# LSTM steps on one core: the residual of h from one scan over threes, whole h of four steps multiplied by GpSimd

## The chip, the cores and the metric

One core of one Trainium2 chip runs the whole program. The metric is the device time of one execution in microseconds (us); smaller is better. The output has the shape of x, 4 sequences of 1024 positions with 512 features.

## What is computed

Four blocks follow one another, each with a residual addition: a sparsifier, an LSTM, a gated recurrence that works by cumulative sums, and a second LSTM. The two LSTMs are the same code with other weights; the change touches them alone.

```python
def step(carry, xw_t):            # both LSTMs, 1024 steps, batch 4, H = 512
    prev_h, prev_c = carry
    a = xw_t + prev_h @ Wh        # Wh: 512 x 2048
    i = sigmoid(a[:, :H]); f = sigmoid(a[:, H:2*H])
    o = sigmoid(a[:, 2*H:3*H]); g = tanh(a[:, 3*H:])
    next_c = f * prev_c + i * g
    next_h = o * tanh(next_c)
    return (next_h, next_c), next_h
x = x + sparsify(x, cond)
x = x + lstm(x, cond, Wx1, Wh1, b1)
x = x + gated_scan(x, cond, ...)
x = x + lstm(x, cond, Wx3, Wh3, b3)
```

## The kernel before

**Layout.** Features lie on the 128 partitions. A hidden vector h of 512 features and 4 sequences is therefore 4 chunks of 128 features by 4 columns: 16 columns. The products run in float16 on TensorE, and to keep precision each value is split into two float16 numbers, a high part and a residual ("low") part. Both Wh and h are split so.

**One step.** The 512 hidden units are handled in two halves, A (chunks 0 and 1, `first`) and B (chunks 2 and 3, `second`), so that the engines can overlap. The gates of a half stand in a PSUM bank each (`PA`, `PB`). The h products (`h_product`, line 404) load h as the stationary operand, 8, 16, 24 or 32 columns in the four steps of a group, and stream 256 columns of Wh. Four matmuls, one for each group of 32 array columns, run beside one another.

TensorE takes, in each step, the products of A's part of h (16 matmuls for gates A, then 12 for gates B), then waits for B's part of h (semaphore `h_b`), then 16 for gates A, which completes them (`gates_a`), and 20 for gates B (`gates_b`), and last some products of x for the following group of four steps (line 397). It starts a step when A's part of h is there (`h_a`).

VectorE (DVE) then turns the gates from PSUM by 32x32 transposes (line 593) into feature order, adds the high and the low row (`both_parts`, line 598), multiplies (`multiply`, line 601), and makes c (`new_c`, line 604). ScalarE (ACT) makes tanh of g, i and f (lines 492 and 499), sigmoid of o (495 and 502), and tanh of c (497 and 504). Then DVE has three operations for each half:

```python
whole_h:  HH  = sig_o * tanh_c                    # float32, line 611
high_h:   hi  = float16(sig_o * 128 * tanh_c)     # line 614
low_h:    lo  = float16(HH * 128 - hi)            # line 619, signals h_a or h_b
```

`sig_o` is a float32 tile in SBUF and `tanh_c` one in PSUM, both contiguous and each one step deep. `H` holds, for every chunk, the 32 float16 columns that the matmul loads, side by side.

**Order of the work.** It is written out by hand, engine by engine, and each engine takes its list in order. On DVE, the operations of A and B are interleaved: `whole_h` and `high_h` of A stand between the second transpose of B and `multiply` of B, and `low_h` of A stands behind the addition of B's o gate.

**Groups of four steps.** A bank holds the gates of four steps (V = 4). After each group GpSimd (POOL) adds whole h of the four steps to x (line 384) and then prepares the float16 parts of x for a later group (`parts_of_x`, lines 350, 351 and 354). HH is double-buffered over groups. A loop round has two groups (eight steps); 128 rounds make the 1024 steps of an LSTM.

Of the kernel before, what the change touches and what calls it, by code (L numbers as in the profile page):

```python
# [250 lines left out]
def lstm(nc, m, tag, x_all, weights, wh, b, wh_there, also_load=()):  # L251
# [7 lines left out]
    with ExitStack() as ctx:  # L259
        s = Sems(nc, ctx, tag, "bias biasd biasp exponent usual sxb xh xscaled xhi xw sq vmax root prep zero br0 ones amaxk amax amaxall cond dbl hi lo next "  # L260
                               "gates_a tr_a to_a pre_a preo_a g_a pr_a c_a tc_a hi_a h_a "
                               "gates_b tr_b to_b pre_b preo_b g_b pr_b c_b tc_b hi_b h_b xadd "
# [4 lines left out]
        H = sbt("H", [P, V, NC, Q], F16)  # L267
        HH = sbt("HH", [P, 2, V, NC * B])
# [18 lines left out]
        class Half:  # L287


            def __init__(self, name, chunk):  # L290
# [13 lines left out]
                self.tanh_c = pst("TC" + name)[:, 0:M]  # L304
                self.sig_o = sbt("SIGO" + name, [P, M])
# [40 lines left out]
        def _(pool):  # L346
# [167 lines left out]
        def _(dve):  # L514
            nc.vector.memset(first.c, 0.0).then_inc(s["zero"], 1)
            nc.vector.memset(second.c, 0.0).then_inc(s["zero"], 1)
            nc.vector.memset(H[:], 0.0).then_inc(s["zero"], 1)
# [103 lines left out]

            with dve.Fori(0, ROUNDS) as r:
                for v in range(2):
                    for u in range(V):
# [296 lines left out]
```

## Time and profile before

| | |
|---|---|
| median of 3 runs | 7913.7 us (7913.2 to 7918.02) |
| the profiled execution's own time | 7913.46 us |
| its span, first to last instruction | 7911.4 us |
| PE busy | 5366.3 us (68%), 169280 matmuls |
| DVE busy | 5627.1 us (71%), 37427 instructions |
| ACT busy | 2281.7 us (29%) |
| POOL busy | 842.9 us (11%) |
| DMA | 37.24 MB, 5 GB/s over the span |

The span is what the profiler saw between the first instruction and the last; 2.06 us of the execution's time lie outside it. PE is the stream of matmuls and PEld the weight loads, which overlap it. Names that begin with p_ belong to the first LSTM and those with q_ to the second; `p_PREA` is A's gates in feature order, `p_GBA` holds A's tanh values and c, `p_PRA` its products, `p_SIGOA` and `p_TCA` its sigmoid of o and tanh of c. DVE and ACT overlap an instruction with the one before it, so an instruction's duration is longer than the distance between two starts. A wait is shown in square brackets or behind a bar, with what ended it.

### The profile page before, as it was taken

To read this page: it belongs to the slowest core of one execution; us is meant where nothing else is said; L and a number is where in the kernel's file an instruction comes from. 1 tells how busy PE (TensorE), PEld (TensorE's weight loads), DVE (VectorE), ACT (ScalarE), POOL (GpSimd) and SP (SyncE) were. 2 spreads that over 40 slices of the span, in tenths; PEclk is the share of its full clock that TensorE was granted. 3 is DMA by queue.
4 is the path that set the end of the run, shared out by engine and by line. 5 is a ranking of instruction groups with operands and counts; after the bars stand their busy time and mean duration, and the time that the engine had idled before them with its cause. 6 is when DMAs were issued, how large, how long until landed. Compare 5 with 4: busy or idle time off the path is not lost. (4 is left out here: it accounts for less than half of the span.)

```text
span 7911.4 us, 404450 instructions
## 1 busy us (share of the span) xinstructions
PE 5366.3 (68%) x169280; PEld 4157.3 (53%) x169280; DVE 5627.1 (71%) x37427; ACT 2281.7 (29%) x12741; POOL 842.9 (11%) x2143
## 2 busy tenths in 40 slices
PE   1566666666666666666983666666666666666666
PEld 1455555555555555555431555555555555555555
DVE  7777777777777777777678777777777777777776
ACT  4322222222222222222354222222222222222222
POOL 5100000000000000000013000000000000000000
PEclk5899999999999999999996999999999999999999
DMA  2000000000000000000001000000000000000001
GB/s 85 17 0 0 0 0 0 0 0 0 0 0 0 0 0 0 0 0 0 0 0 43 0 0 0 0 0 0 0 0 0 0 0 0 0 0 0 0 0 43
DMA packets 32261, 37.24 MB, mean 5 GB/s; under 512 B 6112, under 2 KB 22496, under 8 KB 32224
## 3 DMA queue, kind: packets, MB, share of 16 engines
q1 hardware_dynamic: 32224, 36.76, 1.4%
q8 instruction: 21, 0.34, 0.0%
q14 instruction: 16, 0.13, 0.0%
HBM read 28.34 MB, written 8.39 MB: 5 GB/s over the span
## 5 line engine op out<-in xcount | busy, mean ns | idle before, releaser
L404 PE MATMUL q_PA<-scratch,q_H 128*8 128x256 f16 (+1 forms) x32768 | 1255.2, 273 | 1071.8 <-DVE q_H L619 1071.8
L404 PE MATMUL p_PA<-scratch,p_H 128*8 128x256 f16 (+1 forms) x32768 | 1254.9, 273 | 1071.8 <-DVE p_H L619 1071.8
L404 PEld LDWEIGHTS q_PA<-scratch,q_H 128*8 128x8 f16 (+1 forms) x32768 | 649.7, 90 | 1494.2 <-DVE q_H L619 1359.7
L404 PEld LDWEIGHTS p_PA<-scratch,p_H 128*8 128x8 f16 (+1 forms) x32768 | 649.0, 90 | 1494.6 <-DVE p_H L619 1359.6
L404 PE MATMUL q_PB<-scratch,q_H 128*8 128x256 f16 (+1 forms) x32768 | 1249.7, 273 | 0.0
L404 PE MATMUL p_PB<-scratch,p_H 128*8 128x256 f16 (+1 forms) x32768 | 1249.4, 273 | 0.0
L593 DVE STREAM_TRANSPOSE q_GT<-q_PA 128x192 f32<-128x192 f32 (+1 forms) x2048 | 526.0, 295 | 747.7 <-PE q_PA L404 747.7
L593 DVE STREAM_TRANSPOSE p_GT<-p_PA 128x192 f32<-128x192 f32 (+1 forms) x2048 | 526.5, 295 | 746.7 <-PE p_PA L404 746.7
L404 PEld LDWEIGHTS q_PB<-scratch,q_H 128*8 128x8 f16 (+1 forms) x32768 | 834.5, 92 | 59.8
L404 PEld LDWEIGHTS p_PB<-scratch,p_H 128*8 128x8 f16 (+1 forms) x32768 | 833.5, 92 | 60.8
L492 ACT ACTIVATE q_GBA<-q_PREA 128x24 f32<-128x24 f32 x1024 | 194.7, 190 | 1900.9 <-DVE q_PREA L598 1900.9
L492 ACT ACTIVATE p_GBA<-p_PREA 128x24 f32<-128x24 f32 x1024 | 194.9, 190 | 1900.3 <-DVE p_PREA L598 1900.3
L593 DVE STREAM_TRANSPOSE q_GT<-q_PB 128x192 f32<-128x192 f32 (+1 forms) x2048 | 639.5, 312 | 0.0
L593 DVE STREAM_TRANSPOSE p_GT<-p_PB 128x192 f32<-128x192 f32 (+1 forms) x2048 | 639.4, 312 | 0.0
L384 POOL TENSOR_TENSOR xb<-xb,q_HH 128x64 f32 x256 | 81.9, 320 | 3172.4 <-DVE q_H L619 3172.4
L384 POOL TENSOR_TENSOR xa<-xa,p_HH 128x64 f32 x256 | 81.6, 319 | 3172.7 <-DVE p_H L619 3172.7
L736 PE MATMUL g_z<-xa,scratch 128*128 128x512 f32 x768 | 351.6, 619 | 45.4 <-DVE scratch L788 43.5
L598 DVE TENSOR_TENSOR p_PREB<-p_GT 128x24 f32<-128x24 f32 (+1 forms) x2048 | 361.7, 177 | 0.0
L598 DVE TENSOR_TENSOR q_PREB<-q_GT 128x24 f32<-128x24 f32 (+1 forms) x2048 | 361.5, 177 | 0.0
L619 DVE SCALAR_TENSOR_TENSOR p_H<-p_HH,p_H 128x8 f16<-128x8 f32 x2048 | 334.4, 163 | 35.4
L619 DVE SCALAR_TENSOR_TENSOR q_H<-q_HH,q_H 128x8 f16<-128x8 f32 x2048 | 334.2, 163 | 35.4
L598 DVE TENSOR_TENSOR q_PREA<-q_GT 128x24 f32<-128x24 f32 (+1 forms) x2048 | 359.3, 175 | 0.0
(220 smaller groups left out, 9390.6 us busy)
## 6 DMA issues: line engine op xcount, KB each, us to landing
scratch<-in_x_dram SPq DMA_DIRECT2D x8, 1024.0 KB, 5.4
out_dram<-xa SPq DMA_DIRECT2D x16, 512.0 KB, 6.1
xb<-in_L_cond_Wx_dram SPq DMA_DIRECT2D x8, 384.0 KB, 6.8
xb<-in_L_cond_Wh_dram SPq DMA_DIRECT2D x8, 384.0 KB, 6.7
xa<-in_L_cond_Wx_dram SPq DMA_DIRECT2D x8, 384.0 KB, 5.9
xa<-in_L_cond_Wh_dram SPq DMA_DIRECT2D x8, 384.0 KB, 6.1
xb<-in_L_cond_Wx_dram SPq DMA_DIRECT2D x8, 128.0 KB, 7.0
xb<-in_L_cond_Wh_dram SPq DMA_DIRECT2D x8, 128.0 KB, 6.8
```

The source lines that it names most:

```text
L384: nc.gpsimd.tensor_tensor(here, here, HH[:, v].rearrange("p u (c b) -> p c u b", b=B), ALU.add).then_inc(s["xadd"], 1)
L404: last = nc.tensor.matmul(half.banks[buf][Q * j:Q * j + rows, 0:GA * Q], H[:, u, k, 0:rows], w16[:, part, k, j, half_cols(half)], start=False,
L492: nc.scalar.activation(first.tanhs, first.pre_gif.rearrange("p (n m) -> p n m", n=3), ACT.Tanh, scale=half_scale).then_inc(s["g_a"], 1)
L593: return nc.vector.transpose(GT[:, lo:hi, :].rearrange("p g n -> p (g n)"), half.banks[v][:, (lo - half.at) * Q:(hi - half.at) * Q])
L598: return nc.vector.tensor_tensor(by_unit(dst), GT[:, lo:hi, at:at + B], GT[:, lo:hi, at + B:at + 2 * B], ALU.add)
L619: return nc.vector.scalar_tensor_tensor(nxt[:, :, B:2 * B], by_unit(HH[:, v, u, half.cols]), H_SCALE, nxt[:, :, 0:B], ALU.mult, ALU.subtract)
L736: last = nc.tensor.matmul(banks[w * 2 + n % 2][:], wt[:, w, k, c * P:(c + 1) * P], m.xa[:, k, blk * TBB:(blk + 1) * TBB], start=(k == 0), ...
```

## The change

`sig_o` and `tanh_c` of eight steps now lie in one float32 SBUF tile `SO`, in threes: for each column a zero, sigmoid of o and tanh of c. ACT writes sigmoid and tanh into it, 4 bytes at a time with 12 and 24 bytes between them. `H` becomes a tile `HP` of float16 threes, where the third place holds h and the first place of the high half a constant -128. `high_h` reads `SO` in place of a tile in SBUF and one in PSUM. `low_h` becomes one scan over 24 elements, with state = data0 * state - data1: over a three, it gives 128, then 128 times sigmoid of o, then that times tanh c minus the high part, which is the residual. So it no longer needs `HH`, and `whole_h` is gone from DVE. GpSimd multiplies sigmoid and tanh of the four steps of a group in one instruction and then adds as before. The matmul loads the stationary columns with 12 bytes between them.

```diff
+        HP = sbt("H", [P, 2, V, V, 2, B, NF, 3], F16)
+        SO = sbt("SO", [P, U, 2, B, NF, 3])
+        HH = sbt("HH", [P, V, NC * B])
...
-                self.tanh_c = pst("TC" + name)[:, 0:M]
-                self.sig_o = sbt("SIGO" + name, [P, M])
+                self.n = chunk // NF
+                self.sig_o, self.tanh_c = (SO[:, :, self.n, :, :, e].rearrange("p u b c -> p u c b") for e in (1, 2))
...
-                    nc.gpsimd.tensor_tensor(here, here, HH[:, v].rearrange("p u (c b) -> p c u b", b=B), ALU.add).then_inc(s["xadd"], 1)
+                    nc.gpsimd.tensor_tensor(HH[:].rearrange("p u (h c b) -> p (u h) b c", h=2, b=B),
+                                            *(SO[:, v * V:(v + 1) * V, :, :, :, e].rearrange("p u h b c -> p (u h) b c") for e in (1, 2)), ALU.mult).then_inc(s["whole"], 1)
+                    pool.wait_ge(s["whole"], done)
+                    nc.gpsimd.tensor_tensor(here, here, HH[:].rearrange("p u (c b) -> p c u b", b=B), ALU.add).then_inc(s["xadd"], 1)
...
-                    last = nc.tensor.matmul(half.banks[buf][Q * j:Q * j + rows, 0:GA * Q], H[:, u, k, 0:rows],
+                    last = nc.tensor.matmul(half.banks[buf][Q * j:Q * j + rows, 0:GA * Q], HP[:, k // NF, u, 0:u + 1, :, :, k % NF, 2].rearrange("p u s b -> p (u s b)"),
...
-            nc.vector.memset(H[:], 0.0).then_inc(s["zero"], 1)
+            nc.vector.memset(HP[:].rearrange("p h s u t b c e -> p (h s u t b c) e")[:, :, 0], -H_SCALE).then_inc(s["zero"], 1)
+            nc.vector.memset(HP[:].rearrange("p h s u t b c e -> p (h s u t b c) e")[:, :, 1:3], 0.0).then_inc(s["zero"], 1)
...
-            def whole_h(half, v, u):
-                return nc.vector.tensor_tensor(HH[:, v, u, half.cols], half.sig_o[:], half.tanh_c, ALU.mult)
-
-            def high_h(half, u):
-                return nc.vector.scalar_tensor_tensor(next_h(half, u)[:, :, 0:B], by_unit(half.sig_o[:]), H_SCALE, by_unit(half.tanh_c),
-                                                      ALU.mult, ALU.mult)
+            def high_h(half, v, u):
+                at, here = v * V + u, (u + 1) % V
+                return nc.vector.scalar_tensor_tensor(HP[:, half.n, here, here, 0, :, :, 2].rearrange("p b c -> p c b"), half.sig_o[:, at], H_SCALE,
+                                                      half.tanh_c[:, at], ALU.mult, ALU.mult)
             def low_h(half, v, u):
-                nxt = next_h(half, u)
-                return nc.vector.scalar_tensor_tensor(nxt[:, :, B:2 * B], by_unit(HH[:, v, u, half.cols]), H_SCALE, nxt[:, :, 0:B],
-                                                      ALU.mult, ALU.subtract)
+                here = (u + 1) % V
+                threes = lambda a: a.rearrange("p b c e -> p (b c e)")
+                return nc.vector.tensor_tensor_scan(threes(HP[:, half.n, here, here, 1]), threes(SO[:, v * V + u, half.n]),
+                                                    threes(HP[:, half.n, here, here, 0]), 0.0, ALU.mult, ALU.subtract)
```

**On DVE**, in a step from B's second transpose on, before:

```order
L593 STREAM_TRANSPOSE p_GT<-p_PB 128x64
L611 TENSOR_TENSOR p_HH<-p_SIGOA,p_TCA 128x8 [waits p_tc_a]
L614 SCALAR_TENSOR_TENSOR p_H<-p_SIGOA,p_TCA 128x2x4
L601 SCALAR_TENSOR_TENSOR p_PRB<-p_GBB 128x16 [waits p_g_b]
L598 TENSOR_TENSOR p_PREB<-p_GT 128x8 [waits p_to_b]
L619 SCALAR_TENSOR_TENSOR p_H<-p_HH,p_H 128x2x4 [waits p_hi_a]
L604 SCALAR_TENSOR_TENSOR p_GBB<-p_PRB 128x8 [waits p_pr_b]
L611 TENSOR_TENSOR p_HH<-p_SIGOB,p_TCB 128x8 [waits p_tc_b]
L614 SCALAR_TENSOR_TENSOR p_H<-p_SIGOB,p_TCB 128x2x4
L619 SCALAR_TENSOR_TENSOR p_H<-p_HH,p_H 128x2x4 [waits p_hi_b]
```

and with the change, where `p_SO` is the tile of threes:

```order
L600 STREAM_TRANSPOSE p_GT<-p_PB 128x64
L615 SCALAR_TENSOR_TENSOR p_H<-p_SO 128x2x4 [waits p_tc_a]
L608 SCALAR_TENSOR_TENSOR p_PRB<-p_GBB 128x16 [waits p_g_b]
L605 TENSOR_TENSOR p_PREB<-p_GT 128x8 [waits p_to_b]
L622 SCALAR_TENSOR_TENSOR p_H<-p_SO,p_H 128x24 [waits p_hi_a]
L611 SCALAR_TENSOR_TENSOR p_GBB<-p_PRB 128x8 [waits p_pr_b]
L615 SCALAR_TENSOR_TENSOR p_H<-p_SO 128x2x4 [waits p_tc_b]
L622 SCALAR_TENSOR_TENSOR p_H<-p_SO,p_H 128x24 [waits p_hi_b]
```

The two multiplications of line 611 are gone, and the rest keeps its places. The last instruction of each half, line 619 before and line 622 now, is printed under one name, but is the scan of 24 elements.

**On GpSimd**, at the end of a group of four steps, before:

```order
L384 ISA [waits p_h_b,p_h_a]
L384 TENSOR_TENSOR xa<-xa,p_HH 128x4x16
L350 ISA [waits p_xh,p_xw]
L350 TENSOR_TENSOR p_XC<-xa,p_SXB 128x64
L351 TENSOR_TENSOR p_XH<-xa,p_SXB 128x16x4
```

and with the change:

```order
L387 TENSOR_TENSOR p_HH<-p_SO 128x8x4x2 [waits p_h_b,p_h_a]
L390 ISA [waits p_whole]
L390 TENSOR_TENSOR xa<-xa,p_HH 128x4x16
L353 ISA [waits p_xh,p_xw]
L353 TENSOR_TENSOR p_XC<-xa,p_SXB 128x64
L354 TENSOR_TENSOR p_XH<-xa,p_SXB 128x16x4
```

One instruction is added ahead of the addition to x, it waits for both halves of h, and the addition waits for it. Everything behind, the three instructions that prepare x, comes later by what these take.

## Rows read from the trace of the kernel before

**Rows 1.** Page, groups: count | busy us, mean ns | idle us before

```profile
L593 DVE STREAM_TRANSPOSE p_GT<-p_PA 128x192 f32<-128x192 f32 (+1 forms) x2048 | 526.5, 295 | 746.7 <-PE p_PA L404 746.7
```

**Rows 2.** DVE timeline, one step: start us, us, instruction [idle before <-releaser]

```profile
2003.39 0.51 DVE L593 STREAM_TRANSPOSE p_GT<-p_PA 128x192 f32<-128x192 f32 x2 [0.73 <-PE p_PA L404]
2003.83 0.17 DVE L598 TENSOR_TENSOR p_PREA<-p_GT 128x24 f32<-128x24 f32 x1
...
2004.46 0.17 DVE L604 SCALAR_TENSOR_TENSOR p_GBA<-p_PRA 128x8 f32<-128x8 f32 x1
...
2004.88 0.16 DVE L611 TENSOR_TENSOR p_HH<-p_SIGOA,p_TCA 128x8 f32<-128x8 f32 x1
...
2005.03 0.17 DVE L601 SCALAR_TENSOR_TENSOR p_PRB<-p_GBB 128x16 f32<-128x16 f32 x1
...
2005.19 0.16 DVE L619 SCALAR_TENSOR_TENSOR p_H<-p_HH,p_H 128x8 f16<-128x8 f32 x1
2005.27 0.16 DVE L604 SCALAR_TENSOR_TENSOR p_GBB<-p_PRB 128x8 f32<-128x8 f32 x1
2005.67 0.16 DVE L611 TENSOR_TENSOR p_HH<-p_SIGOB,p_TCB 128x8 f32<-128x8 f32 x1 [0.25 <-ACT p_TCB L504]
...
2005.95 0.17 DVE L619 SCALAR_TENSOR_TENSOR p_H<-p_HH,p_H 128x8 f16<-128x8 f32 x1
2006.83 0.52 DVE L593 STREAM_TRANSPOSE p_GT<-p_PA 128x192 f32<-128x192 f32 x2 [0.72 <-PE p_PA L404]
```

**Rows 3.** Timeline of ACT, the same step

```profile
2004.66 0.18 ACT L497 ACTIVATE p_TCA<-p_GBA 128x8 f32<-128x8 f32 x1
2004.78 0.18 ACT L499 ACTIVATE p_GBB<-p_PREB 128x24 f32<-128x24 f32 x1
...
2005.46 0.18 ACT L504 ACTIVATE p_TCB<-p_GBB 128x8 f32<-128x8 f32 x1
```

**Rows 4.** Timeline of PE, from the start of the next products

```profile
2005.41 0.61 PE L404 MATMUL p_PA<-scratch,p_H 128*8 128x256 f16 x16 [1.09 <-DVE p_H L619]
...
2006.17 0.61 PE L404 MATMUL p_PA<-scratch,p_H 128*8 128x256 f16 x16
```

**Rows 5.** The line of a scan: count, duration ns min/median/max

```profile
L803 DVE TENSOR_TENSOR_SCAN xb<-one,scratch x16: 2292/2294/5972, 3916.7 to 4261.5; 128x1024 f32<-128x1024 f32 x16
```

**Rows 6.** Weight loads by form, 2000 to 3000 us

```profile
L404 PEld LDWEIGHTS p_PB<-scratch,p_H 128*32 128x32 f16 x2304 | 61.6, 97 | 1.2
...
L404 PEld LDWEIGHTS p_PB<-scratch,p_H 128*8 128x8 f16 x2304 | 55.9, 87 | 7.0
```

**Rows 7.** Timeline of PEld, 16 bytes between columns

```profile
7891.79 4.33 PEld L828 LDWEIGHTS s_tp<-ident,xb 128*128 128x128 f32 x35
```

**Rows 8.** Timeline of PEld, contiguous columns

```profile
3799.91 1.78 PEld L725 LDWEIGHTS g_z<-ident,scratch 128*128 128x128 f32 x16
```

**Rows 9.** Groups of ACT, SBUF to SBUF

```profile
L759 ACT ACTIVATE g_LC<-g_LC 128x1024 f32<-128x1024 f32 x16 | 16.9, 1058 | 0.5
...
L487 ACT ACTIVATE p_one_sig<-eps 128x1 f32<-128x1 f32 x1 | 0.2, 203 | 0.0
```

**Rows 10.** Timeline of POOL behind the step of rows 2

```profile
2006.35 0.32 POOL L384 TENSOR_TENSOR xa<-xa,p_HH 128x64 f32 x1 [12.31 <-DVE p_H L619]
...
2006.91 0.32 POOL L351 TENSOR_TENSOR p_XH<-xa,p_SXB 128x64 f16<-128x64 f32 x1
2007.38 0.32 POOL L354 TENSOR_TENSOR p_XH<-p_XC,p_XH 128x64 f16<-128x64 f32 x1
```

**Rows 11.** Timeline of POOL, the next group of four steps

```profile
2020.97 0.32 POOL L351 TENSOR_TENSOR p_XH<-xa,p_SXB 128x64 f16<-128x64 f32 x1
```

**Rows 12.** Timeline of DVE beside rows 11

```profile
2020.64 0.52 DVE L593 STREAM_TRANSPOSE p_GT<-p_PA 128x192 f32<-128x192 f32 x2 [0.72 <-PE p_PA L404]
2021.07 0.26 DVE L598 TENSOR_TENSOR p_PREA<-p_GT 128x24 f32<-128x24 f32 x1
...
2024.20 0.38 DVE L593 STREAM_TRANSPOSE p_GT<-p_PA 128x192 f32<-128x192 f32 x1 [0.73 <-PE p_PA L404]
```

More of the change, by code:

```diff
@@ L261, in lstm @@
                                "gates_a tr_a to_a pre_a preo_a g_a pr_a c_a tc_a hi_a h_a "
-                               "gates_b tr_b to_b pre_b preo_b g_b pr_b c_b tc_b hi_b h_b xadd "
+                               "gates_b tr_b to_b pre_b preo_b g_b pr_b c_b tc_b hi_b h_b xadd whole "
                                + " ".join(f"wh{k}" for k in range(wh_there, NC)))
@@ L266, in lstm @@
         M = NF * B
-        H = sbt("H", [P, V, NC, Q], F16)
-        HH = sbt("HH", [P, 2, V, NC * B])
+        HP = sbt("H", [P, 2, V, V, 2, B, NF, 3], F16)
+        SO = sbt("SO", [P, U, 2, B, NF, 3])
+        HH = sbt("HH", [P, V, NC * B])
         XC = sbt("XC", [P, NC, VB])
@@ L357, in _ @@
             nc.gpsimd.memset(ONES[:], 0.0).then_inc(s["ones"], 1)
-            nc.gpsimd.memset(HH[:], 0.0).then_inc(s["xadd"], 2)
+            nc.gpsimd.memset(SO[:], 0.0).then_inc(s["xadd"], 2)
             pool.wait_ge(s["ones"], 1)
@@ L494, in steps @@
                         act.wait_ge(s["preo_a"], now)
-                        nc.scalar.activation(first.sig_o[:], first.pre_o, ACT.Sigmoid, scale=scale)
+                        nc.scalar.activation(first.sig_o[:, u], by_unit(first.pre_o), ACT.Sigmoid, scale=scale)
                         act.wait_ge(s["c_a"], now)
-                        nc.scalar.activation(first.tanh_c, first.c, ACT.Tanh, scale=0.5).then_inc(s["tc_a"], 1)
+                        nc.scalar.activation(first.tanh_c[:, u], by_unit(first.c), ACT.Tanh, scale=0.5).then_inc(s["tc_a"], 1)
                         act.wait_ge(s["pre_b"], now)
@@ L501, in steps @@
                         act.wait_ge(s["preo_b"], now)
-                        nc.scalar.activation(second.sig_o[:], second.pre_o, ACT.Sigmoid, scale=scale)
+                        nc.scalar.activation(second.sig_o[:, u], by_unit(second.pre_o), ACT.Sigmoid, scale=scale)
                         act.wait_ge(s["c_b"], now)
-                        nc.scalar.activation(second.tanh_c, second.c, ACT.Tanh, scale=0.5).then_inc(s["tc_b"], 1)
+                        nc.scalar.activation(second.tanh_c[:, u], by_unit(second.c), ACT.Tanh, scale=0.5).then_inc(s["tc_b"], 1)
             act.wait_ge(s["usual"], 1)
@@ L586, in _ @@
                 last.then_inc(s["lo"], 1)
-            dve.wait_ge(s["zero"], 3)
-            nc.vector.memset(H[:, 0, 0:NF], 0.0).then_inc(s["h_a"], 1)
-            nc.vector.memset(H[:, 0, NF:], 0.0).then_inc(s["h_b"], 1)
+            dve.wait_ge(s["zero"], 4)
+            nc.vector.memset(HP[:, 0, 0, 0, 0, :, :, 2], 0.0).then_inc(s["h_a"], 1)
+            nc.vector.memset(HP[:, 1, 0, 0, 0, :, :, 2], 0.0).then_inc(s["h_b"], 1)
             def transposed(half, v, cols):
@@ L644, in _ @@
                         dve.wait_ge(s["tc_a"], now)
-                        whole_h(first, v, u)
-                        high_h(first, u).then_inc(s["hi_a"], 1)
+                        high_h(first, v, u).then_inc(s["hi_a"], 1)
                         dve.wait_ge(s["g_b"], now)
@@ L655, in _ @@
                         dve.wait_ge(s["tc_b"], now)
-                        whole_h(second, v, u)
-                        high_h(second, u).then_inc(s["hi_b"], 1)
+                        high_h(second, v, u).then_inc(s["hi_b"], 1)
                         dve.wait_ge(s["hi_b"], now)
```

3 lines of the change are left out of this document (removed).

## The prediction

> **What bounds the kernel now.** I began with the page's groups. DVE is busy 71% of the span, yet at its first transpose of a step it sits idle for PE, 746.7 us in one LSTM's 1024 steps [rows 1], 0.73 us a step. PE has a pause of its own in every step. No engine is full: a loop bounds the kernel, and the timeline of one step shows it. DVE starts A's transpose at 2003.39 and the residual of A's h at 2005.19, ending at 2005.35 [rows 2]. PE takes that h at 2005.41 [rows 4], and its products bring the next transpose at 2006.83 [rows 2]. So a step is 1.96 us on DVE and ACT, 0.06 of handing over and 1.42 on PE, 3.44 in all; 2048 such steps make about 7050 of the span's 7911.4 us. Whatever moves the end of A's `low_h`, seen from the transpose, moves the time 2048-fold: 1 ns a step is 2 us.
>
> What sets that end? Not DVE's own list alone. ACT's tanh c of A ends at 2004.84 [rows 3], and DVE's `whole_h` starts at 2004.88 [rows 2]. The tanh for B's gates ends at 2004.96 [rows 3], and `multiply` of B starts at 2005.03 [rows 2]. The usual distance from ACT's end to DVE's start is 0.03: tanh c of B ends at 2005.64 [rows 3], `whole_h` of B starts at 2005.67 [rows 2]. So `multiply` could have begun at 2004.99. It came 0.04 late, behind `whole_h` and `high_h`.
>
> B's h is level with its need: it is ready at 2006.12, so to PE at 2006.18 [rows 2], and PE's first 28 matmuls last until 2006.17 [rows 4].
>
> **Part by part.** *`whole_h` of A goes.* Small DVE operations start 0.08 apart (2005.19 and 2005.27 [rows 2]), so 0.08 of issue goes. But `multiply` waits for ACT's tanh at 2004.99, so only 0.04 reaches it, and the addition and `low_h` behind it. Bounds: 0 where ACT's tanh comes later, 0.08 where it comes earlier. I take the gain at 0.04.
>
> *The residual becomes a scan.* A scan of 1024 elements takes at least 2292 ns [rows 5]. With a fixed part like that of the small operations (0.16 for 8 elements [rows 2], so about 0.15), it takes (2292 - 150)/1024 = 2.1 ns an element; 24 elements make 0.05, plus 0.15 is 0.20. Before it was 0.16 [rows 2]. Cost 0.04; bounds 0.03 and 0.06, the latter if the fixed part is a little larger for a scan. The next DVE operation, `new_c` of B, starts later than `low_h` by as much more, so it stays where it was, and so does tanh c of B.
>
> *Weight loads with 12 bytes between columns.* The load ahead of a step's first matmul is exposed, the others hide behind matmuls of 109 ns for four (28 in 0.76 us [rows 4]). Contiguous columns cost (97 - 87)/24 = 0.42 ns each [rows 6]. The nearest strided loads, 16 bytes apart, come one in 0.124 us (35 in 4.33), or 0.97 ns a column [rows 7], against 0.111 contiguous (16 in 1.78 [rows 8], which there the matmul sets). The difference, 0.55 ns, times a mean of 20 columns is 0.01 us a step. Bounds 0 and 0.01. The Trainium skill says otherwise ("SBUF — State Buffer", on SBUF cachelines): a stride is free up to 16 bytes, which covers both the 12 bytes here and the 16 of [rows 7]. By the rule this term would be nothing and the sum 20 us less; the row at 16 bytes contradicts it, and I go by the row.
>
> *ACT writes to SBUF, in threes.* Tanh c took 0.18 into PSUM [rows 3]. From SBUF to SBUF ACT takes 203 ns for one element and 1058 for 1024 [rows 9], so about 0.21 for 8: 0.03 more. For A, `high_h` can be 0.03 late and still end before the scan needs it. The following tanh starts 0.12 behind [rows 3]; whether this distance stays is not in the rows: between -0.01 and +0.01, and I take 0. For B: `high_h` starts 0.03 later than `whole_h` did but 0.05 earlier than `high_h` did, and the scan takes back 0.04. B's h stays level with PE's need; 0.
>
> Sum of a step: -0.04 + 0.04 + 0.01 = +0.01, **20 us** in 2048 steps. Bounds: -0.02 (-0.04, +0.03, 0 and ACT's -0.01) and +0.04 (-0.04, +0.06, +0.01, +0.01), which is -41 and +82 us.
>
> *GpSimd.* The new multiplication has 64 elements, as the addition that takes 0.32 [rows 10]; strides may make it longer. It starts once B's h is there. The addition started 0.23 behind B's h (2006.12 [rows 2], 2006.35 [rows 10]). The multiplication starts 0.03 to 0.23 behind, lasts 0.32, and the addition follows 0.23 later: it and all behind it move by 0.35 to 0.55, I take 0.45. DVE never waits for these results, since the x parts are for a later group. But there is a second coupling. In one group of four, POOL's second preparing operation starts at 2006.91, over DVE's transposes, which read PSUM [rows 10, 2]. In the next it starts at 2020.97 [rows 11], 0.33 after DVE's transpose at 2020.64, and the addition of A's gates, which reads two SBUF operands at 2021.07, takes 0.26 instead of 0.17 [rows 12, 2]. That step lasts 3.56 instead of 3.44 [rows 12, 2]. This pair alternates with the two groups of a round; so a hit costs about 0.11 and there is one in eight steps. Moved by 0.45, POOL's three operations start, from the transpose: 0.25, 0.53 and 1.00 in the one group, 0.50, 0.78 and 1.25 in the other. DVE's two-operand work runs from 0.44 (2003.83 [rows 2]) on, nearly without a gap. I count one hit in the first group (the operation at 1.00, on the work around c at 1.07) and two in the second (0.78 and 1.25). That is two hits more in eight steps: 2 x 0.11 x 256 = **56 us**. Bounds: from no hit at all (-28) to four more (+113).
>
> *Setup and tail.* DVE clears 1536 numbers instead of 256, at most 3 us an LSTM at the scan's rate and perhaps hidden; the last group's multiplication adds 0.55 at the end of each LSTM. Together 4 us (0 to 8).
>
> The sum is 20 + 56 + 4 = 80 us on the profiled execution's 7913.46, which is the median within 0.3 us: **7993 us**.
>
> **Rivals.**
>
> *The saved issue counts whole (faster).* Its place is `multiply` of B. If ACT, no longer writing tanh c to PSUM, starts B's tanh enough earlier that it ends by 2004.92, the full 0.08 is saved. The step is then 0.08 - 0.04 - 0.01 = 0.03 shorter, 61 us; with one more hit of GpSimd (28) and the setup (4) the time is 7884. It decides from where the step saves more than GpSimd adds: with 60 us there, 0.03 a step. For it: [rows 3] do not say what holds the tanh at 2004.78. Against: tanh c itself can start no earlier, since it waits for `new_c` (2004.46 to 2004.63 [rows 2], tanh at 2004.66 [rows 3]).
>
> *GpSimd's shift is harmless.* Its operations fall between DVE's, as in the group of [rows 10], and there are as many hits as before. Then 20 + 4 remain: 7937. For it: 0.25 us of shift decides in today's trace between a hit and none. Against: DVE's two-operand work is dense from 0.44 on.
>
> *A hit holds longer.* The addition at 2021.07 [rows 12] ran beside an operation that began 0.10 before it [rows 11] and lost 0.09, not the rest of that operation, 0.22. The Trainium skill ("SBUF — State Buffer", on who interferes with whom) states that the first to issue keeps the shared ports for its whole instruction and the other blocks fully. The rows show less than that. As a mechanism here: each hit costs 0.22, three hits in eight steps less the 0.11 of now make 0.55 x 256 = 141 us, so 7913 + 20 + 141 + 4 = 8078.
>
> *The four weight loads share a reader.* With 32 columns for each of four tiles, a group of four matmuls needs 128 strided columns: 0.12 us instead of 0.109 [rows 7, 4]. The 11 groups ahead of A's gates then add 0.13 in one step of four, 512 x 0.13 = 67 us: 8060. For it: nothing in the rows excludes it; against: only the widest of the four loads would reach this.
>
> *The scan does not do what it says.* A short scan may have start-up that 1024 elements hide. At 0.25 instead of 0.20 it adds 102 us: 8095.
>
> **How the numbers follow.** Chances: forecast 0.42, saved issue whole 0.17, harmless shift 0.18, longer hold 0.10, shared reader 0.08, costlier scan 0.05. A measurement of this kernel can tell 0.2%, 16 us, from no change. Slower takes the forecast nearly whole (0.40), two thirds of the harmless shift (0.11) and the last three (0.23), less a little for gains that offset them: 0.70. Faster is the first rival and a sliver of the others, 0.17; within 0.2% is 0.13. The range leaves out the costlier scan, most of the longer hold and the far side of the faster rival: 7882 to 8070. The forecast's own is 7945 to 8045.
>
> **What the profile would show.** Right: `low_h` as a scan near 0.20; `multiply` of B 0.04 sooner behind the transpose; the first matmul after h longer by up to 0.02 at 32 columns; steps 1 to 3 of a group within 0.02 of 3.44; the first step of both groups stretched, by 0.1 and 0.2, with DVE operations of 0.25 beside POOL's. Wrong: plain steps below 3.42 (the issue was the bound), first steps no longer than now (GpSimd harmless), four-matmul groups farther apart than 0.109, or a scan over 0.22.

## The result and the profile after

| | before | after |
|---|---|---|
| median of 4 runs each | 7913.99 us (7913.2 to 7918.02) | 8009.5 us (8006.59 to 8011.24) |
| ratio, 95% interval | | 1.012 [1.0108, 1.0132] |
| the profiled execution's own time, span | 7913.46, 7911.4 us | 8006.59, 8004.8 us |
| DVE instructions | 37427 | 33333 |
| first matmul on h in the first LSTM | 245.51 us | 247.37 us |

The changed kernel is slower by 95.5 us, 1.2%. DVE has 4094 instructions fewer and is busy 79 us less, and still the loop is longer. All times are of executions in the same state but one: the fourth of experiment 1 took 13980.96 us at a granted clock of 0.44 instead of 0.98, and without it the median there is 7965.5 instead of 7965.9. From the page's groups of the changed kernel:

```profile
PE 5428.4 (68%) x169280; PEld 4377.9 (55%) x169280; DVE 5547.8 (69%) x33333; ACT 2419.8 (30%) x12741; POOL 1023.9 (13%) x2655
...
L600 DVE STREAM_TRANSPOSE p_GT<-p_PA 128x192 f32<-128x192 f32 (+1 forms) x2048 | 526.4, 295 | 763.9 <-PE p_PA L410 763.9
...
L615 DVE SCALAR_TENSOR_TENSOR p_H<-p_SO 128x8 f16<-128x8 f32 x2048 | 381.9, 186 | 320.6 <-ACT p_SO L510 291.4
...
L622 DVE TENSOR_TENSOR_SCAN p_H<-p_SO,p_H 128x24 f16<-128x24 f32 x2048 | 419.4, 205 | 35.4
```

The first transpose of a step now waits 763.9 us for PE in one LSTM instead of 746.7 [rows 1]: 17 ns a step more from PE's side. The scan takes 205 ns, `high_h` 186.

One step without any disturbance, on DVE's timeline of the changed kernel (a step with 32 columns behind it, to be laid beside [rows 2]):

```profile
2009.66 0.51 DVE L600 STREAM_TRANSPOSE p_GT<-p_PA 128x192 f32<-128x192 f32 x2 [0.75 <-PE p_PA L410]
...
2011.18 0.19 DVE L615 SCALAR_TENSOR_TENSOR p_H<-p_SO 128x8 f16<-128x8 f32 x1
2011.27 0.17 DVE L608 SCALAR_TENSOR_TENSOR p_PRB<-p_GBB 128x16 f32<-128x16 f32 x1
...
2011.43 0.20 DVE L622 TENSOR_TENSOR_SCAN p_H<-p_SO,p_H 128x24 f16<-128x24 f32 x1
...
2011.98 0.19 DVE L615 SCALAR_TENSOR_TENSOR p_H<-p_SO 128x8 f16<-128x8 f32 x1 [0.28 <-ACT p_SO L510]
2012.20 0.21 DVE L622 TENSOR_TENSOR_SCAN p_H<-p_SO,p_H 128x24 f16<-128x24 f32 x1
2013.16 0.51 DVE L600 STREAM_TRANSPOSE p_GT<-p_PA 128x192 f32<-128x192 f32 x2 [0.76 <-PE p_PA L410]
```

Seen from its transpose, `multiply` of B starts at 1.61 (1.64 before), A's scan ends at 1.97 (`low_h`: 1.96), and B's scan at 2.75 (`low_h`: 2.73). The step lasts 3.50; at this width it was 3.46 before (the table below), and 3.44 in the narrower step of [rows 2]. ACT and PE in the same step:

```profile
2010.93 0.22 ACT L503 ACTIVATE p_SO<-p_GBA 128x8 f32<-128x8 f32 x1
2011.05 0.18 ACT L505 ACTIVATE p_GBB<-p_PREB 128x24 f32<-128x24 f32 x1
...
2011.72 0.22 ACT L510 ACTIVATE p_SO<-p_GBB 128x8 f32<-128x8 f32 x1
```

```profile
2011.69 0.65 PE L410 MATMUL p_PA<-scratch,p_H 128*32 128x256 f16 x16 [1.10 <-DVE p_H L622]
...
2012.49 0.62 PE L410 MATMUL p_PA<-scratch,p_H 128*32 128x256 f16 x16
```

Tanh c lasts 0.22 instead of 0.18, but the tanh behind it still starts 0.12 later, as in [rows 3]. On PE the first 28 matmuls with 32 columns last 0.80; in the same step before they took 0.78:

```profile
2001.95 0.62 PE L404 MATMUL p_PA<-scratch,p_H 128*32 128x256 f16 x16 [1.09 <-DVE p_H L619]
...
2002.73 0.61 PE L404 MATMUL p_PA<-scratch,p_H 128*32 128x256 f16 x16
```

The weight loads by form (count | busy us, mean ns | idle us before), of 2000 to 3000 us of the changed kernel: 122 ns at 32 columns and 88 at 8, where [rows 6] had 97 and 87.

```profile
L410 PEld LDWEIGHTS p_PB<-scratch,p_H 128*32 128x32 f16 x2272 | 65.3, 122 | 0.0
...
L410 PEld LDWEIGHTS p_PB<-scratch,p_H 128*8 128x8 f16 x2304 | 56.5, 88 | 6.4
```

A table over all steps between 2000 and 3000 us says it more sharply. It holds medians, in ns, of distances between starts, apart for the four widths of the next products. "h to transpose" runs from the first matmul on the new h to DVE's next transpose; B's h is the end of its last operation, counted from that matmul; so are the starts of the second and the eighth group of four matmuls (the eighth is the first that needs B's h); the last column is the period of a step, at 16 columns with the steps that GpSimd lengthens.

| columns | transpose to h matmul | h to transpose | B's h | second group of matmuls | eighth group | period |
|---|---|---|---|---|---|---|
| before, 8 | 2017 | 1426 | 707 | 109 | 764 | 3443 |
| before, 16 | 2074 | 1429 | 707 | 113 | 768 | 3503 |
| before, 24 | 2020 | 1433 | 707 | 116 | 771 | 3453 |
| before, 32 | 2020 | 1437 | 704 | 120 | 775 | 3457 |
| after, 8 | 2031 | 1442 | 716 | 116 | 772 | 3472 |
| after, 16 | 2112 | 1452 | 716 | 126 | 781 | 3561 |
| after, 24 | 2030 | 1466 | 719 | 138 | 793 | 3497 |
| after, 32 | 2031 | 1480 | 721 | 148 | 803 | 3509 |

So a plain step has three additions: about 0.01 at A's h, 0.007 to 0.028 between the first and the second group of four matmuls (the groups behind stay 109 apart: 655 from the second to the eighth at any width), and about 0.01 at B's h and the load behind it. The last shows behind the eighth group: the ninth starts 116, 117, 119 and 123 ns after it at the four widths, where it was 109 before.

What is left is GpSimd. Its timeline at the two group ends of one loop round:

```profile
2002.02 0.31 POOL L387 TENSOR_TENSOR p_HH<-p_SO 128x64 f32<-128x64 f32 x1 [11.86 <-DVE p_H L622]
2002.52 0.32 POOL L390 TENSOR_TENSOR xa<-xa,p_HH 128x64 f32 x1 [0.18 <-POOL p_HH L387]
...
2003.55 0.35 POOL L357 TENSOR_TENSOR p_XH<-p_XC,p_XH 128x64 f16<-128x64 f32 x1
...
2017.38 0.32 POOL L354 TENSOR_TENSOR p_XH<-xa,p_SXB 128x64 f16<-128x64 f32 x1
2017.85 0.36 POOL L357 TENSOR_TENSOR p_XH<-p_XC,p_XH 128x64 f16<-128x64 f32 x1
```

and DVE beside them:

```profile
2002.60 0.52 DVE L600 STREAM_TRANSPOSE p_GT<-p_PA 128x192 f32<-128x192 f32 x2 [0.72 <-PE p_PA L410]
...
2003.67 0.25 DVE L611 SCALAR_TENSOR_TENSOR p_GBA<-p_PRA 128x8 f32<-128x8 f32 x1
...
2006.16 0.51 DVE L600 STREAM_TRANSPOSE p_GT<-p_PA 128x192 f32<-128x192 f32 x2 [0.73 <-PE p_PA L410]
...
2016.63 0.51 DVE L600 STREAM_TRANSPOSE p_GT<-p_PA 128x192 f32<-128x192 f32 x2 [0.73 <-PE p_PA L410]
...
2017.50 0.23 DVE L608 SCALAR_TENSOR_TENSOR p_PRA<-p_GBA 128x16 f32<-128x16 f32 x1
```

In the one group `new_c` takes 0.25 beside POOL's last operation, in the other `multiply` 0.23 beside the one before; their neighbours in the same step keep their 0.16 to 0.18. That is two hits in eight steps, where there was one [rows 11, 12]. The multiplication lasts 0.31, and the addition starts 0.50 behind it.

### The profile page after: what moved, and what is told of

Same layout as the page of the kernel before. It is cut to its first block and busy times, and to the rows that moved or that the text cites. A ratio compares the mean times of both kernels' runs of the same rounds, so it can differ in the third digit from the quotient of the medians.

```text
span 8004.8 us, 400868 instructions
## 1 busy us (share of the span) xinstructions
PE 5428.4 (68%) x169280; PEld 4377.9 (55%) x169280; DVE 5547.8 (69%) x33333; ACT 2419.8 (30%) x12741; POOL 1023.9 (13%) x2655
## 5 line engine op out<-in xcount | busy, mean ns | idle before, releaser
L410 PEld LDWEIGHTS q_PA<-scratch,q_H 128*8 128x8 f16 (+1 forms) x32768 | 730.7, 108 | 1472.4 <-DVE q_H L622 1376.7
L410 PEld LDWEIGHTS p_PA<-scratch,p_H 128*8 128x8 f16 (+1 forms) x32768 | 730.4, 108 | 1472.2 <-DVE p_H L622 1376.6
L600 DVE STREAM_TRANSPOSE p_GT<-p_PA 128x192 f32<-128x192 f32 (+1 forms) x2048 | 526.4, 295 | 763.9 <-PE p_PA L410 763.9
L410 PEld LDWEIGHTS q_PB<-scratch,q_H 128*8 128x8 f16 (+1 forms) x32768 | 890.4, 105 | 23.2
L410 PEld LDWEIGHTS p_PB<-scratch,p_H 128*8 128x8 f16 (+1 forms) x32768 | 890.2, 105 | 23.0
L615 DVE SCALAR_TENSOR_TENSOR p_H<-p_SO 128x8 f16<-128x8 f32 x2048 | 381.9, 186 | 320.6 <-ACT p_SO L510 291.4
L615 DVE SCALAR_TENSOR_TENSOR q_H<-q_SO 128x8 f16<-128x8 f32 x2048 | 381.9, 186 | 320.5 <-ACT q_SO L510 291.4
L387 POOL TENSOR_TENSOR q_HH<-q_SO 128x64 f32<-128x64 f32 x256 | 79.5, 311 | 3079.3 <-DVE q_H L622 3079.3
L387 POOL TENSOR_TENSOR p_HH<-p_SO 128x64 f32<-128x64 f32 x256 | 79.5, 311 | 3078.6 <-DVE p_H L622 3078.6
L622 DVE TENSOR_TENSOR_SCAN q_H<-q_SO,q_H 128x24 f16<-128x24 f32 x2048 | 419.5, 205 | 35.4
L622 DVE TENSOR_TENSOR_SCAN p_H<-p_SO,p_H 128x24 f16<-128x24 f32 x2048 | 419.4, 205 | 35.4
```

The costliest lines, as they stand in the source:

```text
L387: nc.gpsimd.tensor_tensor(HH[:].rearrange("p u (h c b) -> p (u h) b c", h=2, b=B), *(SO[:, v * V:(v + 1) * V, :, :, :, e].rearrange("p u h ...
L600: return nc.vector.transpose(GT[:, lo:hi, :].rearrange("p g n -> p (g n)"), half.banks[v][:, (lo - half.at) * Q:(hi - half.at) * Q])
L615: return nc.vector.scalar_tensor_tensor(HP[:, half.n, here, here, 0, :, :, 2].rearrange("p b c -> p c b"), half.sig_o[:, at], H_SCALE, hal ...
L622: return nc.vector.tensor_tensor_scan(threes(HP[:, half.n, here, here, 1]), threes(SO[:, v * V + u, half.n]), threes(HP[:, half.n, here, h ...
```

## The experiments

Two accounts were open after this. **Mine**: a plain step costs 0.01 and GpSimd 56 us. **The other**: the plain step costs about 0.04, in tiles of threes that are slower for every engine that touches them, and GpSimd adds little. The runs take one part of the change away, or put one part into the kernel before. Each ratio is to the kernel before, timed on the same chip beside it (7912.04 for the first four, 7916.11 for the next four, 7910.2 for the last two). It moved by 6 us between these, so that a difference between kernels of two sets is good to some 5 us.

**1. The changed kernel, with contiguous weight loads**

```diff
-  HP[:, k // NF, u, 0:u + 1, :, :, k % NF, 2].rearrange("p u s b -> p (u s b)")
+  HP[:, k // NF, u].rearrange("p v s b c e -> p (v s b c e)")[:, 0:rows]
```

> The changed kernel, but TensorE loads its stationary columns side by side (the same number, other values of the same tile, so h is wrong). Theory A (strided weight loads are the largest part of the loss): in the changed kernel the second group of four matmuls follows the first of a step by 116, 126, 138 and 148 ns at 8, 16, 24 and 32 columns, against 109 to 120 before; here it is 109 to 120 again, the second exposed load (behind the wait for B's h) shrinks too, steps 1 to 3 of a group fall by 10 to 35 ns, and the time is about 7960. Rival B (the loads only look longer, the loss sits in DVE and ACT): the time stays above 7995.

Measured: 7965.88 us, ratio 1.0067 [1.0047, 1.0087]. So the strides in the weight loads cost 44 us, 0.021 a step, twice my term. The loads are back at their old 97 ns:

```profile
L410 PEld LDWEIGHTS p_PB<-scratch,p_H 128*32 128x32 f16 x2304 | 61.6, 97 | 1.2
```

and the second group starts after 109 to 120 ns as before. The distance from h to transpose is 1433 at 8 columns and 1444 at 32, still 7 longer than before: this is B's h, 715 instead of 707.

**2. The changed kernel, without GpSimd's multiplication**

```diff
-  nc.gpsimd.tensor_tensor(HH[:]..., *(SO[...] for e in (1, 2)), ALU.mult).then_inc(s["whole"], 1)
-  pool.wait_ge(s["whole"], done)
...
+  nc.gpsimd.memset(HH[:], 0.0).then_inc(s["whole"], 1)
```

> The changed kernel without GpSimd's multiplication; the addition to x adds zeros, so h is left out of the output. Theory A (GpSimd's share is small: the first step of a group grew by about as much as the other three): between 7995 and 8015, with one hit per two groups as in the kernel before. Rival C (the prediction's term: two hits more in eight steps are 56 us): about 7953.

Measured: 7992.13 us, ratio 1.0101 [1.0084, 1.0118]. Without the multiplication 17 us go, not 56, and the time is 3 us below the range that I gave. The multiplication is the small part of the loss. GpSimd's own operations are then back where they were before the change: in one group the step with 16 columns lasts 3589 ns in the mean, in the other 3480, so one group in two is hit, by 0.11, as before.

**3. The changed kernel, with the residual as an operation of 8 elements**

```diff
-  return nc.vector.tensor_tensor_scan(threes(HP[...1]), threes(SO[...]), threes(HP[...0]), 0.0, ALU.mult, ALU.subtract)
+  return nc.vector.scalar_tensor_tensor(h(1), half.sig_o[:, at], H_SCALE, h(0), ALU.mult, ALU.subtract)
```

> The changed kernel with an 8-element operation in place of the 24-element scan, with the same tiles and strides (it leaves tanh c out of the residual, so that is wrong). Theory A: low_h goes from 0.20 to about 0.16, h of A and of B both come 0.04 sooner, and the time falls by 2048 x 0.04 = 82 us to about 7928, near the kernel before: then scan and saved multiplication cancel and the rest of the loss is elsewhere. Rival D (the scan is hidden behind waits): above 7980.

Measured: 7946.96 us, ratio 1.0043 [1.0026, 1.006]. I expected 7928, from the scan's 205 ns against 163 for the old `low_h`. The group shows why less came back:

```profile
L622 DVE SCALAR_TENSOR_TENSOR p_H<-p_SO,p_H 128x8 f16<-128x8 f32 x2048 | 373.9, 183 | 35.5
```

In these tiles even 8 elements take 183 ns. Of the 42 ns that the scan takes more than the old operation, the strides account for 20 and the 24 elements for 22.

**4. The changed kernel, with whole h back on DVE**

```diff
-  HH = sbt("HH", [P, V, NC * B])
+  HH = sbt("HH", [P, 2, V, NC * B])
...
+  def whole_h(half, v, u):
+      at = v * V + u
+      return nc.vector.tensor_tensor(by_unit(HH[:, v, u, half.cols]), half.sig_o[:, at], half.tanh_c[:, at], ALU.mult)
...
+  whole_h(first, v, u)
...
+  whole_h(second, v, u)
```

> The changed kernel's tiles, strides and scan, but whole_h is back on DVE ahead of high_h in both halves and GpSimd only adds. Theory A: in the changed kernel multiply of B follows high_h of A directly (0.089 after its start), so the operation put back costs its whole issue distance of 0.09 for A, and the step grows by 0.08 to 0.09: 8170 to 8195. Rival E (only 0.04 reaches the path, as the prediction took for the saving): about 8090.

Measured: 8334.49 us, ratio 1.0534 [1.0516, 1.0551], far above what I expected. PE's timeline has both halves of it:

```profile
2001.34 0.64 PE L407 MATMUL p_PA<-scratch,p_H 128*24 128x256 f16 x16 [1.18 <-DVE p_H L623]
...
2002.19 0.37 PEld L407 LDWEIGHTS p_PA<-scratch,p_H 128*24 128x24 f16 x16 [0.15 <-DVE p_H L623]
```

PE waits for A's h 1.18 instead of 1.10, and then 0.15 more for B's h. Over 1000 us, the transpose to the h matmul has a median of 2113 ns (2030 in the changed kernel), B's h 804 (719) and h to transpose 1549 (1466), all at 24 columns. So the operation costs 0.08 at A and 0.08 again at B. I had counted A alone: B's wait had no slack left. In this layout the step from `whole_h` on DVE to the multiplication on GpSimd is worth 325 us. It is worth so much because in this layout tanh c ends later and `high_h` waits for it: `multiply` of B then starts 0.09 behind `high_h`, with no wait for ACT left in which another operation could hide. In the kernel before it still started 0.04 behind the point where ACT let it. What the same step would be worth in the contiguous layout was not run. The next three runs measure what the layout costs in the kernel before.

**5. The kernel before, with h in strided columns only**

```diff
-  H = sbt("H", [P, V, NC, Q], F16)
+  H = sbt("H", [P, V, NC // NF, Q, NF, 3], F16)
...
-  H[:, u, k, 0:rows],
+  H[:, u, k // NF, 0:rows, k % NF, 2],
```

> The kernel before, with 12 bytes between the stationary columns of h and nothing else changed. Theory A (each of the two loads that PE has to wait out in a step, behind h of A and behind h of B, costs 0.9 ns more a column): the second group of four matmuls at 116, 126, 138 and 148 ns after the first, a step 0.02 to 0.03 longer, 7953 to 7975. Rival B (loads hidden or only the first 0.01 exposed, as the prediction took): 7912 to 7934.

Measured: 8024.28 us, ratio 1.0136 [1.0119, 1.0153]: 108 us where I expected about 50. The loads do what they do in the changed kernel, 122 ns. The rest is in DVE, which writes and reads h in the same columns:

```profile
L404 PEld LDWEIGHTS p_PB<-scratch,p_H 128*32 128x32 f16 x2272 | 65.3, 122 | 0.0
```

```profile
L614 DVE SCALAR_TENSOR_TENSOR p_H<-p_SIGOA,p_TCA 128x8 f16<-128x8 f32 x1024 | 177.6, 173 | 0.0
...
L619 DVE SCALAR_TENSOR_TENSOR p_H<-p_HH,p_H 128x8 f16<-128x8 f32 x2048 | 373.6, 182 | 35.2
```

`high_h` went from 155 to 173 ns and `low_h` from 163 to 182. Transpose to the h matmul is 2037 to 2039 ns instead of 2017 to 2020 (at 8, 24 and 32 columns), and h to transpose 22 to 49 longer.

**6. The kernel before, with tanh c in SBUF, contiguous**

```diff
-  self.tanh_c = pst("TC" + name)[:, 0:M]
+  self.tanh_c = sbt("TC" + name, [P, M])[:]
```

> The kernel before, with tanh c in a contiguous SBUF tile in place of PSUM. Theory A (ACT takes about 0.02 to 0.03 longer into SBUF, and both halves feel it, since DVE waits for tanh c of A and PE for h of B): a step 0.03 to 0.05 longer, 7970 to 8015. Rival F (the destination costs nothing, the strides do): within 10 of 7912.

Measured: 8058.56 us, ratio 1.018 [1.0163, 1.0197]. One tile moved from PSUM to SBUF costs 142 us, and the time is above the range that I gave.

```profile
L497 ACT ACTIVATE p_TCA<-p_GBA 128x8 f32<-128x8 f32 x1024 | 213.7, 209 | 0.0
```

Tanh c takes 209 ns instead of 180, and in this kernel everything behind it is queued on it: transpose to the h matmul is 2056 instead of 2017, B's h 742 instead of 707 (at 8 columns). The Trainium skill ("ScalarE: Activation LUTs", section "Step-by-step: what each stage is for") says that PSUM is the lower-latency destination for this engine. The 180 and 209 ns agree.

**7. The kernel before, with sigmoid of o and tanh c in threes**

```diff
+  SO = sbt("SO", [P, U, 2, B, NF, 3])
...
-  self.tanh_c = pst("TC" + name)[:, 0:M]
-  self.sig_o = sbt("SIGO" + name, [P, M])
+  self.n = chunk // NF
+  self.sig_o, self.tanh_c = (SO[:, :, self.n, :, :, e].rearrange("p u b c -> p u c b") for e in (1, 2))
```

> The kernel before, with sigmoid of o and tanh c in the SBUF tile of threes (12 and 24 bytes between elements), but whole_h and the 8-element low_h as before, and h contiguous for PE. Theory A (tanh c 0.216 instead of 0.18, whole_h and high_h 0.01 to 0.03 longer with 0.09 between starts instead of 0.08, in both halves): a step 0.08 to 0.10 longer, 8075 to 8120. Rival F (only the strides of ACT's writes count): about 7912 + 2048 x 0.036, 7986.

Measured: 8133.05 us, ratio 1.0274 [1.0257, 1.0292].

```profile
L498 ACT ACTIVATE p_SO<-p_GBA 128x8 f32<-128x8 f32 x1024 | 221.5, 216 | 0.0
```

```profile
L612 DVE TENSOR_TENSOR p_HH<-p_SO 128x8 f32<-128x8 f32 x2048 | 353.6, 173 | 318.4 <-ACT p_SO L505 288.9
```

The threes add 7 ns to tanh c beyond SBUF itself, and DVE reads them more slowly: 173 ns for `whole_h`, 161 to 163 before. It is 217 us in all (13 us above the range that I gave), and experiment 6 explains 142 of them.

**8. The kernel before, with GpSimd's preparation of x spread over steps.** Its first two operations together, and the third by itself, wait for B's h of a later step, so that they start while DVE waits for PE:

```diff
-  def parts_of_x(x, buf, n):
+  def parts_of_x(x, buf, n, later=None):
...
+      if later is not None:
+          pool.wait_ge(s["h_b"], later)
...
-  parts_of_x(xt_ahead[:, :, bass.ds(r * UB + v * VB, VB)], v, pool.snap(r * 2 + (v + 3)))
+  pool.wait_ge(s["h_b"], pool.snap(r * U + (v * V + 2)))
+  parts_of_x(xt_ahead[:, :, bass.ds(r * UB + v * VB, VB)], v, pool.snap(r * 2 + (v + 3)), pool.snap(r * U + (v * V + 3)))
```

> The kernel before, with GpSimd's preparation of x held back: its first two operations start when h of B of the first step of a group is there, the third when that of the second step is, so that all run while DVE waits for PE or transposes. Theory A (a GpSimd operation beside DVE's two-operand work costs 0.11 in one of eight steps, and nothing else does): no step is stretched, 7912 - 256 x 0.11 = 7884. Rival G (the stretched step comes from the loop round or from the PE products added in that step): 7912, and the stretched step stays.

Measured: 7886.9 us, ratio 0.9963 [0.9948, 0.9977]. This beats both kernels, and it measures GpSimd's hits in the kernel before: 29 us. The step with 16 columns falls from 3503 to 3449 ns, the other widths stay. POOL's timeline, and the first transposes of DVE beside it:

```profile
1999.86 0.32 POOL L387 TENSOR_TENSOR xa<-xa,p_HH 128x64 f32 x1 [6.75 <-DVE p_H L622]
2003.24 0.32 POOL L350 TENSOR_TENSOR p_XC<-xa,p_SXB 128x64 f32<-128x64 f32 x1 [3.06 <-DVE p_H L622]
2003.53 0.32 POOL L351 TENSOR_TENSOR p_XH<-xa,p_SXB 128x64 f16<-128x64 f32 x1
2006.59 0.32 POOL L356 TENSOR_TENSOR p_XH<-p_XC,p_XH 128x64 f16<-128x64 f32 x1 [2.74 <-DVE p_H L622]
```

```profile
2000.34 0.52 DVE L596 STREAM_TRANSPOSE p_GT<-p_PA 128x192 f32<-128x192 f32 x2 [0.72 <-PE p_PA L407]
...
2003.79 0.51 DVE L596 STREAM_TRANSPOSE p_GT<-p_PA 128x192 f32<-128x192 f32 x2 [0.73 <-PE p_PA L407]
...
2007.24 0.52 DVE L596 STREAM_TRANSPOSE p_GT<-p_PA 128x192 f32<-128x192 f32 x2 [0.73 <-PE p_PA L407]
...
2010.70 0.51 DVE L596 STREAM_TRANSPOSE p_GT<-p_PA 128x192 f32<-128x192 f32 x2 [0.73 <-PE p_PA L407]
```

Every operation of POOL ends at the latest 0.06 after the start of DVE's first transpose, and no step is longer than the others: they start 3.45 apart.

**9. The changed kernel, with the same spreading**

The edit of experiment 8, in the changed kernel.

> The changed kernel, with GpSimd's preparation of x held back to the first and second step of the group. Theory A (the changed kernel has two hits in eight steps, which stretch two steps by 0.053 and 0.083 over the 3.488 of the same step without one): 8009.5 - 256 x 0.136 = 7975, still slower than both kernels that load h side by side. Rival C (GpSimd is the main part of the loss, 56 us or more): below 7955.

Measured: 7962.96 us, ratio 1.0068 [1.0051, 1.0085]. The changed kernel's distance from the kernel before, each timed beside it, shrinks from 95.5 to 52.8 us, so GpSimd's hits cost it 43 us (I expected 35), against 29 before: the change added 14. The periods of the four widths are now 3467, 3480, 3492 and 3507 ns, with no lengthened step. Against experiment 8, 76 us of the plain step and the setup remain (82 if each is taken from its own neighbour).

**10. The changed kernel, with the operation of 8 elements in half B alone**

```diff
+  if half is second:
+      at, here = v * V + u, (u + 1) % V
+      h = lambda part: HP[:, half.n, here, here, part, :, :, 2].rearrange("p b c -> p c b")
+      return nc.vector.scalar_tensor_tensor(h(1), half.sig_o[:, at], H_SCALE, h(0), ALU.mult, ALU.subtract)
```

> The changed kernel with an 8-element operation in place of the scan in half B alone (it leaves tanh c out of B's residual, so that is wrong). Theory A (PE waits for h of B: the eighth group of four matmuls after a step's start comes 7 to 14 ns late): h of B comes 0.02 sooner, that wait falls to nothing or nearly, A's side stays, and a step is 0.005 to 0.012 shorter: 7984 to 8000. Rival H (B's h is hidden behind PE's first 28 matmuls): within 5 of 8009.

Measured: 7989.38 us, ratio 1.0101 [1.0084, 1.0118]. B's scan alone is worth 20 us; together with experiment 3, A's is worth 42. A's scan is paid in full, 0.02 a step. B's returns half of its 0.02, and this shows that PE did wait for B's h in the changed kernel. The place shows too: with the strided loads kept, the ninth group of matmuls is back at 109 ns behind the eighth at every width.

## Why the prediction was right in its sign and wrong in its parts

The time, 8009.5, lies 16 us above the forecast of 7993. The parts do not agree like that: the plain step's term was 20 us and is about 80, and GpSimd's was 56 and is about 15. The two errors nearly cancelled, which is luck. By the table's periods a step grew by 29 ns at 8 columns and by 52 at 32; with the part from transpose to matmul about 10 longer and the part from h to transpose 16, 23, 33 and 43 longer for the four widths (29 in the mean), it is 39 ns. 2048 times that is 80 us; with GpSimd's 14 and the 2 to 4 of the setup that makes 96 to 98, and 95.5 were measured. By the signs that the prediction gave, steps 1 to 3 of a group should have stayed within 0.02 of 3.44; they last 3.47 to 3.51, and that alone says that its plain step was too cheap.

Step by step:

- **`whole_h` of A, -0.04.** `multiply` of B came 0.03 sooner behind the transpose, not 0.04 (1.61 for 1.64). Right. The missing 0.01 is tanh c's, below. The issue of 0.08 is not saved whole: the rival that counted it so is out.
- **The scan, +0.04.** 205 ns for 163. Right, but half by accident: the 24 elements make 22 of the 42 and the strides the other 20 (experiment 3). The costlier scan is out. At A the two terms leave the 0.01 of the table.
- **Weight loads, +0.01, bounds 0 and 0.01.** Under-sized, and the first step that failed. I took 0.97 ns a column from loads of float32 16 bytes apart [rows 7]. With 12 bytes and float16, a column costs (122 - 88)/24 = 1.42 ns, where contiguous it was 0.42. Times a mean of 20 columns that is 0.020 more, and the second group of matmuls starts 7, 13, 22 and 28 ns later than before, 0.0175 in the mean. A second load, the one behind the wait for B's h, is exposed while B's h is late: against experiment 1 its strides add about 1 ns up to 24 columns and 7 at 32, and with B's h sooner (experiment 10) nothing. Experiment 1 puts both at 44 us. The Trainium skill ("SBUF — State Buffer", on SBUF "cachelines") gives the distance that one can stride for free as 4 values of float32 or 8 of two bytes, which is 16 bytes. Neither these loads nor DVE's writes in experiment 5 (155 to 173 ns at 12 bytes) bear this out. The same note of the Trainium skill wants at least two accesses in each line of 16 bytes, which columns 12 bytes apart mostly do not give. That half, which the prediction left out, would have led one to expect the cost.
- **ACT into SBUF, +0.03 on tanh c, 0 on the path.** The duration was right in kind (209 contiguous, 216 to 218 in threes, for 180). For A the path took 0.01 of it, not the 0 that I wrote. I looked only at whether `high_h` ends before the scan needs it. But `multiply` of B is next in DVE's list: `high_h` starts 1.52 behind the transpose, where tanh c lets it, and `multiply` 0.09 later at 1.61, while ACT's tanh for B's gates would have let it start at 1.60.
- **"B's h stays level with PE's need; 0".** The second step that failed. I let `high_h` keep its 0.155. It takes 0.186 in the tiles of threes, and the scan waits for its end. So: `high_h` 0.05 earlier, 0.03 longer, the scan 0.04 longer, which makes the 0.02 that B's h came late behind the transpose, 0.01 of it relative to the matmul (9 to 17 ns). Since PE had no slack there (I had found h and PE level myself), a late B is paid at once: 7 ns a step in experiment 1, where the loads are contiguous, and experiment 10 gets its part back. The premise stood in the prediction; the conclusion, a zero, did not follow from it.
- **GpSimd, +56.** The mechanism was right, the count and the price were not. I expected the first group's last operation to strike at 1.00 behind the transpose and found it at 0.95, striking `new_c`. In the second group I expected two hits, at 0.78 and at 1.25; the one at 0.75 strikes `multiply`, the one at 1.22 starts together with an addition of DVE and lengthens nothing there (POOL's own operation takes 0.36 instead of 0.32). And a hit costs 0.09 in the first group and 0.06 in the second, not 0.11: the step with 16 columns lasts 3571 and 3540 ns in the mean, and 3480 where GpSimd's work is spread (experiment 9). The 0.11 of before was 0.09 at the addition and 0.02 at `multiply` behind it, in the same step. Experiments 8 and 9 moved GpSimd's operations to where DVE waits or transposes, and the hits went.
- **The longer hold.** Its price of 0.22 is out, and so is its 8078; its mechanism is not, and the prediction was wrong to take [rows 11, 12] as evidence against it. What is lost is not the rest of POOL's operation, since DVE's own 0.17 run beside it. What tells is where DVE's operation ends. In [rows 11, 12] it ends at 2021.33 and POOL's at 2021.29; in the changed kernel `new_c` ends at 2003.92 and POOL's at 2003.90, `multiply` at 2017.73 and POOL's at 2017.70. Experiment 3 happens to place an addition of 8 elements 0.02 behind POOL's start, and it takes 0.33 instead of 0.17 (13 of the changed kernel's groups have the same):

```profile
2017.82 0.32 POOL L357 TENSOR_TENSOR p_XH<-p_XC,p_XH 128x64 f16<-128x64 f32 x1
```

```profile
2017.84 0.33 DVE L605 TENSOR_TENSOR p_PREA<-p_GT 128x8 f32<-128x8 f32 x1
```

  Over the traces of all kernels but the two of experiments 8 and 9 there are some 4800 such cases. DVE's operation is 147 to 159 ns longer where it starts 20 to 32 ns behind POOL's, 49 to 100 at 100 to 137 ns, and 17 to 27 at 151 to 158 ns; and in every one of them it ends 19 to 50 ns after POOL's. So DVE's operation is held until POOL's is over or nearly so. Where DVE's starts 19 ns or less behind, it keeps its length within 15 ns, and POOL's takes 0.36 instead of 0.32. The Trainium skill ("SBUF — State Buffer", section "Who interferes with whom") has the first to issue keep the ports for its whole instruction while the other blocks. The traces agree.
- **A shared reader of the four weight loads.** Out: from the second to the eighth group of matmuls it is 655 ns at 8 and at 32 columns, before and after.
- **Setup, +4.** The first matmul of h came 1.9 us later in the first LSTM, as its memsets are 912 and 485 ns instead of 272 (1536 float16 numbers for 512; the 256 of the prediction are words of 32 bits); the end of each LSTM was not measured by itself.

The change is thus a trade: the tiles of threes cost DVE, ACT and PE together 0.21 us a step, the scan's 24 elements among it (experiment 4, which has all of this with `whole_h` on DVE, stands 422 us above its kernel before), and the multiplication taken from DVE gives back 0.16. Contiguous weight loads and the spreading together were not run; if their 44 and 43 to 46 us add, the changed kernel would come to about 7920 to 7923, an estimate, and so still not below the 7887 of experiment 8.

## What to carry to other kernels

A layout chosen to make one instruction possible is paid by every instruction that touches the tile, on every engine; price each of them, in ns, before the one that is saved. Where a buffer is ready just as it is needed, no term on it is zero: write what 10 ns late costs. When work on GpSimd cannot hurt by being late, give it waits that put it where VectorE is idle: this alone gave 29 us in the one kernel and 43 in the other. And to judge whether one instruction holds another, compare their ends, not how much longer the second became.

## What the runs showed of the hardware that was not expected

- A weight load from float16 columns 12 bytes apart costs 1.42 ns a column, against 0.42 contiguous (122 and 97 ns at 32 columns, 88 and 87 at 8).
- Eight float16 values written by DVE at a stride of 12 bytes cost 18 to 19 ns more than side by side (155 to 173 for `high_h`, and 163 to 182 for `low_h`, which also reads such values); in the changed kernel `high_h`, which also reads float32 in threes, goes to 186.
- ACT's activation of 8 elements takes 180 ns from SBUF to PSUM, 177 from PSUM to SBUF, 209 from SBUF to SBUF, and 216 to 218 from SBUF where the destination is in threes.
- The next activation starts 0.12 behind tanh c whether that takes 0.18 or 0.22: the longer duration costs only whoever waits for the result.
- A small operation of DVE with two SBUF operands that starts 0.02 to 0.16 behind an operation of POOL ends 0.02 to 0.05 after POOL's end, so it is 0.16 to 0.02 longer, the more the sooner it starts. Where it starts within 0.019, DVE's keeps its length and POOL's takes 0.36 instead of 0.32.
- After a wait for new columns, the distance from the first group of four matmuls to the second carries the length of the weight load (116 to 148 ns at 8 to 32 strided columns, 109 to 120 contiguous); the groups behind it start 109 apart at any width.
